# Attention scores as bf16 products over three-part queries and keys

## What is computed

```python
qkv = (x @ qkv_w.T + qkv_b).reshape(B, T, 3, H, dh)
scores = jnp.einsum('bhtd,bhsd->bhts', q, k) * scale
scores = jnp.where(causal, -jnp.inf, scores)
attn = jax.nn.softmax(scores, axis=-1)
seq_out = jnp.einsum('bhts,bhsd->bhtd', attn, v)
```

## Time and profile before

| | |
|---|---|
| runs | 792.54, 794.30, 796.17 us |
| the profiled execution, its own time | 792.37 us |
| its span in the profile | 790.6 us |
| PE busy | 710.8 us (90%), 4004 matmuls |
| DVE busy | 579.9 us (73%) |
| POOL busy | 425.1 us (54%) |
| ACT busy | 356.5 us (45%) |
| DMA queue q1 | 89.09 MB, 34.2% of 16 engines |

### The profile page before, as it was taken

One profiled execution on the slowest core, in us unless ns is written; L12 is line 12 of the kernel. 1 busy time (PEld: TensorE's weight loads), 2 busy tenths in 40 slices (PEclk: granted clock), 3 DMA queues, 4 the chain that ended last, 5 costly groups with the idle time before them and its releaser, 6 DMA issues.

```text
span 790.6 us, 12236 instructions
## 1 busy us (share of the span) xinstructions
PE 710.8 (90%) x4004; PEld 494.2 (63%) x4004; DVE 579.9 (73%) x1946; ACT 356.5 (45%) x758; POOL 425.1 (54%) x335
## 2 busy tenths in 40 slices
PE   6898999998989999999989968789989999899995
PEld 3465665665656666666656635467767677676774
DVE  2347767869888888888887758447877777777784
ACT  2323555565555565655646648522324233242311
POOL 9300899997586868686868932431504224051320
PEclk9997999999999999999999996879999999999998
DMA  8786453524334324335233352022031230303000
GB/s 286 246 269 214 156 179 130 180 82 143 127 107 170 115 97 158 111 103 193 76 118 133 114 151 80 10 98 80 1 107 35 73 107 1 108 3 105 28 27 27
DMA packets 60084, 89.87 MB, mean 114 GB/s; under 512 B 7898, under 2 KB 36980, under 8 KB 60020
## 3 DMA queue, kind: packets, MB, share of 16 engines
q1 hardware_dynamic: 60020, 89.09, 34.2%
HBM read 54.72 MB, written 33.82 MB: 112 GB/s over the span
## 4 chain that ended last, share of the span: by engine, by line
PE 53%; DVE 23%; ACT 7%; issue 5%; DMA 5%; POOL 5%; SPq 2%; ACTq 0%; POOLq 0%; DVEq 0%
PE ps L1254 16%; PE ps L374 8%; PE ps L327 8%; PE ps L338 7%; PE ps L315 6%; DVE ps L476 5%; DVE Ob L514 3%; DVE A L1388 3%; PE ps L231 2%; DMA qk_scratch<-HL 2%; ACT Pr L412 2%; PE ps L1219 2%; ACT X L1240 2%; ACT Osb L432 1%; DVE Z L1274 1%
## 5 line engine op out<-in xcount | busy, mean ns | idle before, releaser
L476 DVE CUSTOM_DVE_ANT_0 ps<-ps,mask 128x256 f32<-128x256 f32 (+3 forms) x512 | 238.0, 512 | 84.5 <-PE ps L315 83.3
L412 ACT ACTIVATE Pr<-ps 128x512 f32<-128x512 f32 (+2 forms) x384 | 187.9, 524 | 94.0 <-PE ps L327 86.5
L327 PE MATMUL ps<-Q,K 98*128 98x256 f32 (+2 forms) x512 | 173.3, 380 | 13.8 <-ACT Pr L412 11.3
L1254 PE MATMUL ps<-ew_hi,XT 128*128 128x512 f32 x512 | 176.5, 403 | 0.0
L315 PE MATMUL ps<-K,Q 96*128 96x256 f32 (+2 forms) x512 | 151.7, 342 | 20.5 <-DVE nmax L476 20.0
L610 POOL TENSOR_SCALAR_AFFINE_SELECT Pr<-Pr 128x512 f32<-128x512 f32 x128 | 90.6, 723 | 136.1 <-ACT Pr L412 133.4
L1388 DVE SCALAR_TENSOR_TENSOR A<-ps,cw,A 128x256 f32<-128x256 f32 x256 | 123.6, 483 | 47.2 <-PE ps L1254 33.9
L327 PEld LDWEIGHTS ps<-Q,K 98*128 98x128 f32 x512 | 91.3, 193 | 68.7 <-ACT Pr L412 38.2
L315 PEld LDWEIGHTS ps<-K,Q 96*128 96x128 f32 x512 | 99.6, 196 | 37.0 <-DVE nmax L476 20.9
L1254 PEld LDWEIGHTS ps<-ew_hi,XT 128*128 128x128 f32 x512 | 97.3, 190 | 21.3 <-issue 0.3
L1254 PE MATMUL ps<-ew_rest,XT 128*128 128x512 f32 x256 | 101.6, 397 | 0.0
(11 more groups left out here) (191 smaller groups left out, 1030.6 us busy)
## 6 DMA issues: line engine op xcount, KB each, us to landing
qk_scratch<-HL SPq DMA_DIRECT2D x32, 512.0 KB, 2.7
Q<-qk_scratch SPq DMA_DIRECT2D x96, 128.0 KB, 2.7
K<-qk_scratch SPq DMA_DIRECT2D x96, 128.0 KB, 2.8
Pr<-xT SPq DMA_DIRECT2D x8, 512.0 KB, 5.4
xraw<-xT SPq DMA_DIRECT2D x8, 512.0 KB, 4.3
mem_scratch<-Rl SPq DMA_DIRECT2D x16, 256.0 KB, 3.8
mv_scratch<-MV SPq DMA_DIRECT2D x32, 128.0 KB, 1.7
Wm<-mem_scratch SPq DMA_DIRECT2D x2, 2048.0 KB, 9.3
```

Of the source, the lines that this page charges most:

```text
L327: last = nc.tensor.matmul(o, K[0:STACK + 2, hh, P * kt:P * kt + P], Q[0:STACK + 2, hh, T - n:T], start=True, stop=True)
L412: nc.scalar.activation(probs(g % 2, kt, heads[0], len(heads)), src, ACT.Exp, scale=SCALE).then_inc(s_exp, 1)
L476: last = nc.vector.tensor_tensor_reduce(out=scores, in0=scores, in1=mask[:, T - w:T], scale=1.0, scalar=NEG, op0=ALU.add, op1=ALU.max, acc ...
L1254: last = nc.tensor.matmul(o, lhs(c, k), rhs(d, k), start=first, stop=(k == KT - 1 and c == 1))
```

## The change

Queries and keys become bf16 tiles in three parts: high, second and third, each the bf16 of what is left. Six terms (hi·hi, hi·2nd, 2nd·hi, 2nd·2nd, hi·3rd, 3rd·hi) of 16 dimensions fill all 96 rows, so a group's stack takes twelve DMAs of 1 KB rows in place of six of 2 KB rows, and the zero fill goes. The second part is a new ScalarE operation (`act_second`, u = 0 of groups 1 and 2, u = 6 of groups 0 and 1), the third a new POOL operation (`pool_third`, ahead of a mask); VectorE's difference goes to a f32 tile `R`. `HL` is doubled, `qk_scratch` holds three bf16 parts, and each piece has its own semaphore for its write. Products of scores take their exact width, down to 128 columns. The two rows of maxima are bf16. The stack of group 0 is issued in two halves, and the writes of pieces move in SP's order.

```diff
@@ -18,6 +18,8 @@
...
+Q_PARTS, K_PARTS = (0, 0, 1, 1, 0, 2), (0, 1, 0, 1, 2, 0)
+TERMS = len(Q_PARTS)
@@ -57,7 +59,7 @@
...
-    qk_scratch = nc.dram_tensor("qk_scratch", [NB, 4, P, 2, T], F32, kind="Internal").ap()
+    qk_scratch = nc.dram_tensor("qk_scratch", [NB, 4, P, 3, T], BF16, kind="Internal").ap()
@@ -108,15 +110,17 @@
...
-        Q = sb("Q", [P, H, T], F32R, part2)
-        K = sb("K", [P, H, T], F32R, part2)
+        spare = sb("spare", [P, H * T - 3 * T], F32, part2)
+        HL = sb("HL", [P, 2, 3, T], BF16, part2)
+        Q = sb("Q", [P, H, T], BF16, part2)
+        K = sb("K", [P, H, T], BF16, part2)
...
-        MT = sb("MT", [GROUP * QT, 2, 2, P], F32R, part2)
+        MT = sb("MT", [GROUP * QT, 2, 2, P], BF16, part2)
@@ -305,9 +312,9 @@
         def pe_max_scores(pe, b, g, u):
...
-            n = max(P * (i + 1), 2 * P)
+            n = P * (i + 1)
...
-                need(pe, s_stack[g], 96, b, 96)
+                need(pe, s_stack[g], 32 * TERMS, b, 32 * TERMS)
@@ -317,13 +324,13 @@
...
         def pe_exp_scores(pe, b, g, u):
...
-            n = max(T - P * kt, 2 * P)
+            n = T - P * kt
...
-                o = ST_ps[u % 2][:, c * 256:c * 256 + n]
+                o = ST_ps[u % 2][:, c * n:c * n + n]
@@ -361,7 +368,8 @@
...
-            need(pe, s_lo, 8, b, j)
+            need(pe, s_r, 4, b, min(j, 4))
+            need(pe, s_lo, 4, b, max(j - 4, 0))
@@ -407,17 +415,16 @@
...
-            n = max(w, 2 * P)
-            src = ST_ps[u % 2][:, 0:len(heads) * n].rearrange("p (h t) -> p h t", h=len(heads))[:, :, n - w:n]
+            src = ST_ps[u % 2][:, 0:len(heads) * w].rearrange("p (h t) -> p h t", h=len(heads))
...
         def act_project(act, b, j):
...
-                need(act, s_scr[(j - 1) % 4 // 2], 32, b, (0, 16, 32, 16)[j])
+                need(act, s_scr[(j + 2) % 4], 16, b, 16 * (j // 2))
...
-                nc.scalar.activation(HL[:, 0, :], J_ps[:], ACT.Identity, bias=qkb[:, m:m + 1]).then_inc(s_hi, 1)
+                nc.scalar.activation(HL[:, j % 2, 0, :], J_ps[:], ACT.Identity, bias=qkb[:, m:m + 1]).then_inc(s_hi, 1)
@@ -425,6 +432,10 @@
...
+        def act_second(act, b, j):
+            need(act, s_r, 4, b, j + 1)
+            nc.scalar.activation(HL[:, j % 2, 1, :], R[:, j % 2, :], ACT.Identity).then_inc(s_h2, 1)
...
         def act_out(act, b, g):
@@ -454,6 +465,10 @@
...
+                    if g in (1, 2) and u == 0 and not last:
+                        act_second(act, b + 1, 2 * g - 1)
+                    if g < 2 and u == 6 and not last:
+                        act_second(act, b + 1, 2 * g)
@@ -482,13 +497,14 @@
...
-                nc.vector.scalar_tensor_tensor(HL[:, 1, :], J_ps[:], qkb[:, m:m + 1], HL[:, 0, :].bitcast(F32),
-                                               ALU.add, ALU.subtract).then_inc(s_lo, 1)
+                need(dve, s_h3, 4, b, j - 1)
+                nc.vector.scalar_tensor_tensor(R[:, j % 2, :], J_ps[:], qkb[:, m:m + 1], HL[:, j % 2, 0, :],
+                                               ALU.add, ALU.subtract).then_inc(s_r, 1)
...
         def dve_turned_max(dve, b, g):
...
-            nc.vector.tensor_tensor(MT[:, g % 2, 1, :], M_ps[0:GROUP * QT, 0:P], MT[:, g % 2, 0, :].bitcast(F32),
+            nc.vector.tensor_tensor(MT[:, g % 2, 1, :], M_ps[0:GROUP * QT, 0:P], MT[:, g % 2, 0, :],
...
         def dve_normalise(dve, b, g):
@@ -611,35 +627,40 @@
...
+        def pool_third(pool, b, j):
+            need(pool, s_h2, 4, b, j + 1, apart=True)
+            nc.gpsimd.tensor_tensor(HL[:, j % 2, 2, :], R[:, j % 2, :], HL[:, j % 2, 1, :],
+                                    ALU.subtract).then_inc(s_h3, 1)
...
         def sp_load_x(sp, b):
...
         def sp_projected(sp, b, j):
...
-                need(sp, s_lo, 8, b, j + 1, apart=True)
-                sp.dma_start(qk_scratch[b, j], HL[:].bitcast(F32)).then_inc(s_scr[j // 2], 16)
+                need(sp, s_h3, 4, b, j + 1, apart=True)
+                sp.dma_start(qk_scratch[b, j], HL[:, j % 2]).then_inc(s_scr[j], 16)
...
-        def sp_stack(sp, b, g):
+        def sp_stack(sp, b, g, which=(0, 1)):
...
-            half = g // 2
-            need(sp, s_scr[half], 32, b, 32, apart=True)
...
-            for t, dst, parts in ((0, Q, (0, 0, 1)), (1, K, (0, 1, 0))):
-                src = qk_scratch[b, 2 * half + t][r0:r0 + GROUP * DH].rearrange("(h d) s t -> s d h t", h=GROUP)
-                for r, part in enumerate(parts):
-                    sp.dma_start(dst[r:STACK:STACK // DH, GROUP * g:GROUP * g + GROUP, :].bitcast(F32),
+            for t in which:
+                j = 2 * (g // 2) + t
+                need(sp, s_scr[j], 16, b, 16, apart=True)
+                src = qk_scratch[b, j][r0:r0 + GROUP * DH].rearrange("(h d) s t -> s d h t", h=GROUP)
+                for r, part in enumerate((Q_PARTS, K_PARTS)[t]):
+                    sp.dma_start((Q, K)[t][r:STACK:TERMS, GROUP * g:GROUP * g + GROUP, :],
...
         def sp_max_rows(sp, b, g):
...
-                    "o h (i t) -> o (h i) t", i=QT).bitcast(F32), MT[:, g % 2, r, :].bitcast(F32)).then_inc(s_mrow[g], 16)
+                    "o h (i t) -> o (h i) t", i=QT), MT[:, g % 2, r, :]).then_inc(s_mrow[g], 16)
...
         def sp_out(sp, b):
@@ -649,28 +670,35 @@
...
-                if g and not last:
+                if g == 1 and not last:
+                    sp_stack(sp, b + 1, 0, (0,))
+                if g > 1 and not last:
...
+                if g in (1, 2) and not last:
+                    sp_projected(sp, b + 1, 2 * g - 1)
...
-                if not last:
+                if g > 1 and not last:
...
+                if g == 1 and not last:
+                    sp_stack(sp, b + 1, 0, (1,))
...
-                    sp_projected(sp, b + 1, 2 * g + 1)
+                    sp_projected(sp, b + 1, 2 * g + (g > 1))
...
-                    sp.wait_ge(s_lo, NB * 8)
+                    sp.wait_ge(s_lo, NB * 4)
...
-                        sp.wait_ge(s_scr[j], 32 * NB)
+                    for j in range(4):
+                        sp.wait_ge(s_scr[j], 16 * NB)
@@ -714,18 +742,24 @@
...
             def project(j):
-                sp_projected(sp, 0, j)
-                if j == 3:
-                    sp.wait_ge(s_cst, 1)
-                if 3 <= j < 7:
+                if j >= 4:
+                    sp_projected(sp, 0, j)
+                if 4 <= j < 7:
...
+            def memory(i):
+                sp_memory(sp, i)
+                if 2 <= i < 6:
+                    sp_projected(sp, 0, i - 2)
+                if i == 5:
+                    sp_stack(sp, 0, 0)
...
             def mem_rows(c, w0, n, dst):
...
-            opening(project, lambda i: sp_memory(sp, i), lambda: None, lambda u: None)
+            opening(project, memory, lambda: None, lambda u: None)
@@ -786,6 +817,10 @@
...
             def masks(*which):
...
+                    if b < NB - 1 and kt == 0 and g in (1, 2):
+                        pool_third(pool, b + 1, 2 * g - 1)
+                    if b < NB - 1 and kt == 1 and g < 2:
+                        pool_third(pool, b + 1, 2 * g)
...
             def lines(dst, a0, c0, shift, place, flip, between):
@@ -812,6 +847,8 @@
             def group_masks(b, g):
...
+            for j in range(4):
+                pool_third(pool, 0, j)
@@ -903,7 +940,12 @@
...
-            opening(lambda j: act_project(act, 0, j), lambda i: act_memory(act, i), fold, lambda u: None)
+            def memory(i):
+                act_memory(act, i)
+                if 2 <= i < 6:
+                    act_second(act, 0, i - 2)
...
+            opening(lambda j: act_project(act, 0, j), memory, fold, lambda u: None)
```

18 lines of the change are left out of this document (9 added, 9 removed).

## The result

| | before | after |
|---|---|---|
| median of 4 runs each on one chip | 794.55 us | 822.8 us |
| all runs | 792.54 to 796.17 | 815.8 to 823.32 |
| ratio (95% interval) | | 1.0336 (1.0276 to 1.0397) |
| profiled execution: own time, span | 792.37, 790.6 | 823.05, 821.3 |

The forecast was 805 (789 to 818). The sign was right; the loss is 28 us where 11.5 were forecast, and the time lies outside the range. Four runs, three of the kernel before beside experiments 5 to 8 and one of experiment 17, fell in a slower state of the chip (816 to 1120 us) and are left out of all medians.

A forecast was written before the change was run, and what follows sets the result against it. It took TensorE, VectorE and ScalarE handing over to bound batches 2 to 7, POOL 112 to 165 us, SP's queue the opening. Terms 10 + 9.5 + 3 + 2 - 11 - 2 = plus 11.5 on 794.3 gave 805.8, said as 805 (789 to 818).

The forecast's parts named there:

- products of scores: TensorE's score products in batches 2 to 7: narrower bf16 products and shorter open loads gain 11 us, ends 5 and 26.
- waits on HL that go: ScalarE no longer waits for the write of the piece before: minus 2 us, ends 0 and 5.
- seconds on ScalarE, batches 2 to 6 included: Second parts on ScalarE, four a batch, have room; with the thirds plus 2 us for five batches, ends 0 and 8.
- thirds: 9.5 + 3 in batches 0 and 1, the rest in the +2: POOL's thirds: plus 9.5 of work, plus 3 through SP's new wait, and a share of plus 2 in batches 2 to 6.
- twelve DMAs, the opening: Opening, SP queue: 24 more issues delay the first maxima rows and exponents, plus 10 us, ends 0 and 12.
- the term was 16: Products of scores if fast weight load leaves narrow products bound by their own columns: cut 16%, gain 16 us.
- The wait in SP: Writes of pieces 1 and 3 wait for POOL's third, maxima rows behind: nothing in steady batches, plus 3 us from batch 1.
- The third part: Thirds on POOL: plus 9.5 us where POOL is the bound; room in batches 2 to 6, plus 2 together with seconds.
- Plus 9.5: Batches 0 and 1, where POOL is the bound: seven thirds of 1.36 us each, ends 7 and 12.
- plus 3: Batch 1: maxima rows for group 2 wait in SP behind the third and its write, 3 us lost, ends 0 and 6.
- The third, SP and POOL bounding every batch: Rival: maxima rows come 1 to 2 us late in two groups of each batch, 818 us, chance 0.15.

The follow-up runs named there:

- experiments 5 to 8: Changed kernel with six DMAs and no thirds, 785.8 us; maxima rows ahead of gated write, 820.2; that with six DMAs, 803.3; plus thirds of batches 1, 2 on VectorE, 795.1.
- experiment 17: Changed kernel with six DMAs a stack, maxima rows ahead of the gated write, thirds of batches 1 and 2 on VectorE, four HL and R buffers: 797.1 us.
- e2: Kernel before with bf16 types and exact product widths, two parts, six DMAs, no second or third operations: 781.8 us, ratio 0.987.
- e13: Changed kernel with six DMAs a stack and neither second nor third parts computed: 781.4 us.
- e5: Changed kernel with six DMAs a stack and POOL's third parts left out: 785.8 us, ratio 0.990.
- e1: Changed kernel with six DMAs for a stack in place of twelve, by a new layout of dimensions and heads: 809.7 us.
- e4: Changed kernel with POOL's third parts left out, their rows zero, twelve DMAs kept: 805.4 us.
- e11: Kernel before with one stack loaded for two groups, half the DMAs at twice the size: 899.5 us.
- e14: Changed kernel with six DMAs for each stack of batch 0 and twelve for each stack of later batches: 809.6 us.
- e12: Changed kernel with six DMAs; POOL does operations like the thirds on tensors of its own that nobody waits for, low rows zero: 795.9 us.
- e7: Changed kernel with six DMAs a stack and the next group's rows of maxima issued ahead of the gated write: 803.3 us.
- e9: Changed kernel with six DMAs, maxima rows ahead of the gated write, and all 28 thirds of the steady program on VectorE: 811.8 us.
- e3: Kernel before with each of a stack's six DMAs split in two of two heads: 834.6 us.

## Why the prediction was wrong, point by point

Set beside the forecast's terms, the runs read along one path (kernel before, e2, e13, e5, e1, change):

| term of the sum | forecast | measured |
|---|---|---|
| products of scores | -11 | -12.0 (e2) |
| waits on HL that go | -2 | -0.3, nothing: e13 less e2 |
| seconds on ScalarE, batches 2 to 6 included | a part of +2 | +4.3 (e5 less e13) |
| thirds: 9.5 + 3 in batches 0 and 1, the rest in the +2 | about +14 | +23.9 (e1 less e5) |
| twelve DMAs, the opening | +10 | +13.1 (change less e1), 11.1 by first exponents |
| sum | +11.5 | +29 |

The sum starts from 793.8, the kernel before beside e2; against the 794.55 of the result it is 28. The last two terms depend on the path: taken in the other order, by e4, twelve DMAs cost 19.6 and thirds 17.4, since some 6.5 us are waits that either causes. On either path both are above what I gave them.

**Products: right, in size.** The question left open, whether the load binds the narrow ones, has its row now. In PE's timeline of the changed kernel:

```profile
283.07 0.38 PE L334 MATMUL ps<-Q,K 98*128 98x512 bf16 x1
283.29 0.38 PE L322 MATMUL ps<-K,Q 96*128 96x256 bf16 x2
...
286.76 0.28 PE L322 MATMUL ps<-K,Q 96*128 96x128 bf16 x2
286.87 0.33 PE L334 MATMUL ps<-Q,K 98*128 98x384 bf16 x1
```

From 283.07 to 283.29 are 0.22 us for 512 columns, forecast as 0.213. Two products of 128 columns take 0.11 from 286.76 to 286.87, 0.055 each: bound by their own columns, not by a load of 0.11. The Trainium skill, "TensorE: Matmul & The Clock Gate", section on fast weight load, has such a load made in four parallel chunks, and the trace agrees: 101 ns a load where f32r showed 193. By it the term was 16, and the runs gave 12. Why not more was not tried apart. In e2 VectorE is busy 48.77 us of 55 from 220 to 275 us, and the granted clock over batches 2 to 6 is 0.97 where the kernel before has 0.99.

**Opening: right.** Place, cause and size (first exponents forecast for 78, seen at 79.5) hold. That the queue was the tight one before is only half so: e11 took twelve issues away and gained nothing.

**The wait in SP: right that the queue costs nothing in steady batches** as long as thirds are there (e14), though the chain of waits of the changed kernel puts 8.8% on it. Without thirds it costs some 3 us in batches 2 to 6 (e4 less e5).

**The failed step is "The third part", in its sentence on batches 2 to 6.** I read "POOL has room (41.24 of 55)" and let 0.4 us of 7.9 a batch come through, 2 us in all. In batches 2 to 6 the thirds cost 9.8 us (280.6 less 270.8; with twelve DMAs 5.3, e4), 6.9 of them (277.7 less 270.8) in the run where nobody waits for them, and the seconds about 4.3 in all. My reading, not shown, is that the room on POOL is not spread evenly: its outer products and scans pass to VectorE and back in strict order, and a third placed there delays scans that VectorE must do ahead of its maxima. That thirds also make VectorE's own operations longer shows in one row. VectorE's scan of 128 x 512 has a mean of 1298 ns before and 1279 in e5, but 1402 in e12 and 1383 in the changed kernel:

```profile
L530 DVE TENSOR_TENSOR_SCAN Ob<-sc,Ob 128x512 f32<-128x512 f32 x36 | 49.8, 1383 | 1.0 <-POOL Ob L876 1.0
```

36 of them are 3.7 us longer than in e5, in e12 4.4. How much of the 6.9 comes through this and how much through the order was not tried apart.

**A second failed step: batches 0 and 1 by instruction counts.** "Plus 9.5" counted seven thirds by 1.36, and "plus 3" the gate in SP. With six DMAs the thirds cost 11.3 us there (118.3 less 107.0), near the 12.5 I had. But my mechanism was wrong. The share of e12 is 4.5 us where I had 9.5, and waiting for the third is 6.8 where I had 3. Taking the rows of maxima out from behind the gate gives back only 2.7 of that (115.6 in e7, 118.3 in e1). In the changed kernel these batches lose 14.2.

**Waits that go: wrong.** Nothing was gained by them (e13 and e2); ScalarE even has a new one of 5.6 us in batch 1 in the changed kernel.

**The rivals.** The third, SP and POOL bounding every batch, at 818 with chance 0.15, was the nearest. Its place was half right: POOL, not SP. The range left out that several losses lie on the high side at once.

## What to carry to other kernels

An engine with a quarter of its time free is not a free place for small work when it passes data back and forth in strict order. Of 39 us of thirds on POOL (32 by 1.215) 24 us came through in the whole time, 10 of them with nobody waiting for the result; of 20 us of seconds on ScalarE about 4.3. The two engines were 84% and 59% busy from 220 to 275 us, and that alone tells neither. Where an engine is late as a whole, moving one wait behind it gained between nothing clear and 6.4 us here, more buffers gained nothing, and moving its work away gained 8.2; but where the moved work met POOL's long operations it lost 16.7 (e9). Before moving work to another engine, look at what the two do at the same moment. And what a part costs depends on what else is late: the same 24 issues a batch cost 13 us in the opening and nothing after it beside the thirds, but some 6 us after it without them.

## What the runs showed that I had not expected

- A chain of waits charges what it passes through, not what would be saved. It gave SP's stack issues 8.8% of 337 us, 30 us; taking half of them away in e1 gained nothing in batches 2 to 6 (279.2 and 280.6).
- A load of 128 bf16 columns shows 101 ns against 193 for f32r, and does not bound a product of 128 columns, which starts every 0.055 us.
- The third is shorter on VectorE than on POOL, 0.68 us against 1.16 where the other engine is at rest or in other operations, and yet its mean of 28 is 1395 ns against 1215. Beside a two-tensor operation of the other engine either may stand until that one is done: the third on VectorE up to 7.07 us (e9), the one on POOL at 208.43 us of the changed kernel 2.14, beside a scan that VectorE began at 208.41.
- Twelve DMAs a stack cost 41 us with a single HL buffer (e3) and 13 with a doubled one: I take it that the buffer, not the queue, set the price in steady batches. This is argued from the waits of e3; the kernel before with a doubled buffer and twelve DMAs was not tried, and the 13 hold with thirds in place (19.6 without).
- TensorE's granted clock was lower in the versions in which it waited more: over batches 0 and 1 it is 0.95 before with 101 us busy of 106, and 0.88 in the changed kernel with 98 of 120. Part of the 14 us that these batches lost may be this. It is not what the thirds cost: e5 has 0.91 there and e1 0.90, some 19 and 24 us at the lower level, which can make at most 2.5 of the 11.3 us between them, and in batches 2 to 6 e1 has the higher clock (0.98 and 0.97). No run separates it for the products.
